# Both layer norms of a fused attention and mixture-of-experts layer: 16 small VectorE operations each made into two wide ones

## The reference

```python
# layernorm: (x - mean) / sqrt(var + 1e-5) over the 1024 channels
x = x + attn(layernorm(x))      # retention: (q k^T * decay) v, 16 heads of 64,
                                # group norm per head, plus silu(x w1), then @ w2
x = x + ffn(layernorm(x))       # router softmax, top 2 of 8 experts (all 8 computed,
                                # weights 0 elsewhere), plus a gated shared expert
```

## Time and profile before

| | us |
|---|---|
| median of 3 runs | 1963.68 (1962.49 to 1967.89) |
| the profiled execution | 1961.56 |
| its span, slowest core | 1959.8 |
| spans of the eight cores | 1945.3 to 1959.8 |
| PE busy / DVE busy / ACT busy | 1543.4 / 844.4 / 394.5 |

### The profile page before, as it was taken

One profiled execution on the slowest core, in us unless ns is written; L12 is line 12 of the kernel. 1 busy time (PEld: TensorE's weight loads), 2 busy tenths in 40 slices (PEclk: granted clock), 3 DMA queues, 4 the chain that ended last, 5 costly groups with the idle time before them and its releaser, 6 DMA issues.

```text
span 1959.8 us, 21098 instructions; the slowest of 8 cores (1945.3 to 1959.8 us)
## 1 busy us (share of the span) xinstructions
PE 1543.4 (79%) x7156; PEld 619.1 (32%) x7156; DVE 844.4 (43%) x1534; ACT 394.5 (20%) x771; POOL 24.9 (1%) x34
## 2 busy tenths in 40 slices
PE   0565677676576662999899999999999999999960
PEld 0121122122112111444343444444444444443420
DVE  0376666666657655222223333333333333332333
ACT  2433142233323111111121111111111111111100
POOL 1000000000000000000000000000000000000000
PEclk9755665575576565999999999999999999999985
DMA  9000020002000005200502202222220312223015
GB/s 145 2 1 1 0 43 1 0 1 44 1 0 22 1 1 108 44 1 1 86 1 44 44 1 47 40 44 44 43 44 1 53 34 43 44 44 65 1 61 175
DMA packets 41353, 67.27 MB, mean 34 GB/s; under 512 B 3858, under 2 KB 16530, under 8 KB 41250
## 3 DMA queue, kind: packets, MB, share of 16 engines
q0 software_dynamic: 26432, 48.65, 15.3%
q1 hardware_dynamic: 14818, 17.29, 2.7%
HBM read 101.96 MB, written 12.58 MB: 58 GB/s over the span
## 4 chain that ended last, share of the span: by engine, by line
PE 60%; DMA 15%; DVE 15%; issue 5%; DVEq 3%; ACT 2%; POOL 0%; ACTq 0%; SPq 0%; POOLq 0%
PE P L1206 18%; PE P L1238 17%; DMA we_sb<-we 11%; PE P L624 3%; PE P L867 3%; PE P L1071 3%; PE P L1124 3%; PE P L1082 3%; PE P L671 3%; DVE scr L363 2%; DMA xj<-x 2%; DMA x1rl<-x1s 2%; DVE s_sb L655 1%; DVEq L838 1%; PE P L426 1%
## 5 line engine op out<-in xcount | busy, mean ns | idle before, releaser
L1206 PE MATMUL P<-x2st,we_sb 128*128 128x512 bf16 x2048 | 454.2, 383 | 8.5 <-DMA we_sb<-we 8.5
L1238 PE MATMUL P<-htil,we_sb 128*128 128x512 bf16 x1984 | 435.9, 381 | 10.3 <-DMA we_sb<-we 10.3
L1217 ACT ACTIVATE hs_scr<-P 128x512 bf16<-128x512 f32 x256 | 152.9, 597 | 772.4 <-PE P L1206 772.4
L1250 DVE TENSOR_TENSOR acc<-acc,P 128x512 f32<-128x512 f32 x248 | 170.5, 687 | 256.9 <-PE P L1238 256.9
L1206 PEld LDWEIGHTS P<-x2st,we_sb 128*128 128x128 bf16 x2048 | 199.5, 99 | 255.5 <-issue 25.3
L1238 PEld LDWEIGHTS P<-htil,we_sb 128*128 128x128 bf16 x1984 | 194.2, 98 | 248.1 <-issue 17.1
L1224 DVE TENSOR_TENSOR htil<-hs_scr,bcomb 128x512 bf16<-128x512 bf16 x256 | 108.8, 425 | 353.9 <-ACT hs_scr L1217 353.9
L426 PE MATMUL P<-xlnj,w1a_sb 128*128 128x512 bf16 x256 | 79.4, 458 | 48.8 <-DVE xlnj L386 47.8
L624 PE MATMUL P<-qt,kst 64*128 64x512 bf16 x128 | 75.1, 599 | 33.8 <-ACT ktok L561 27.0
L648 DVE SCALAR_TENSOR_TENSOR s_sb<-P,gmn_sb,masks_sb 128x512 bf16<-128x512 f32 (+3 forms) x128 | 70.4, 550 | 72.1 <-PE P L630 65.0
L671 PE MATMUL P<-s_sb,vst 128*64 128x512 bf16 (+3 forms) x128 | 58.6, 458 | 29.3 <-DVE s_sb L655 28.5
(11 more groups left out here) (165 smaller groups left out, 1286.2 us busy)
## 6 DMA issues: line engine op xcount, KB each, us to landing
we_sb<-we POOLq DMA_DIRECT2D x16, 2048.0 KB, 14.6
out<-acc SPq DMA_DIRECT2D x4, 2048.0 KB, 8.0
xj<-x POOLq DMA_DIRECT2D x4, 1024.0 KB, 25.0
x1s<-xj SPq DMA_DIRECT2D x4, 1024.0 KB, 5.3
wgu_sb<-wgu POOLq DMA_DIRECT2D x1, 4096.0 KB, 30.2
x1rl<-x1s SPq DMA_DIRECT2D x4, 1024.0 KB, 10.3
w1a_sb<-w1a POOLq DMA_DIRECT2D x1, 2048.0 KB, 22.6
w2a_sb<-w2a POOLq DMA_DIRECT2D x1, 2048.0 KB, 35.3
```

The lines of the kernel that those rows point to most:

```text
L1206: last = e.matmul(bank[:, :], we1_sb[:, 1024 * k + 128 * f:1024 * k + 128 * f + 128], x2st[:, ST * k + 512 * j:ST * k + 512 * j + 512], st ...
L1217: e.activation(hs_scr[:, hsl:hsl + 512], bank[:, :], AF.Silu),
L1238: last = e.matmul(bank[:, :], we2_sb[:, 1024 * f + 128 * m:1024 * f + 128 * m + 128], htil[:, pslot + 512 * f:pslot + 512 * f + 512], star ...
L1250: e.tensor_add(acc[:, ST * m + 512 * pj:ST * m + 512 * pj + 512], acc[:, ST * m + 512 * pj:ST * m + 512 * pj + 512], bank[:, :]),
```

## The change

`ln_partB` is rewritten. Two new bf16 tiles in SBUF, `bcmu` and `bcrs` (128 x 512), take the spread mean and the reciprocal deviation: ACT copies the mean out of PSUM (new line 360), and DVE's reciprocal writes to `bcrs` in place of PSUM (new line 364). Instead of 16 operations on 512 columns there are two on 4096: one subtraction of `bcmu` (new line 384), one multiplication with `bcrs` (new line 387). The 512 columns of `bcmu` and `bcrs` are read eight times over, by a dimension of stride 0. All operands of both are bf16 in SBUF. LN1 subtracts into `xlnj` and multiplies in place; LN2 subtracts into the slot of `xlnj` that belongs to the same block and multiplies into `x2st`. `scr16` isn't used there any more. All eight marks that the function returns are that of the multiplication. The copy on ACT waits for the multiplication of the layer norm before, the LN2 subtraction for the last residual sum of its block.

```diff
@@ -203,6 +203,8 @@
     masks_sb = sb("masks_sb", [128, 1280], BF16)
     gmn4_sb = sb("gmn4_sb", [128, 64], F32)
     lgb = sb("lgb", [128, 320], F32)
+    bcmu = sb("bcmu", [128, 512], BF16)
+    bcrs = sb("bcrs", [128, 512], BF16)
     combT = sb("combT", [32, ST], BF16)
     eye_sb = sb("eye_sb", [128, 128], BF16)
     rout_sb = sb("rout_sb", [128, 72], BF16)
@@ -345,7 +347,8 @@
                 m_fin = p.do("scalar", fin, waits=[m_var, m_eps], mark=True)
                 return (st_b, m_fin, xoff, Mark("m_vector", m_var.value))
 
-            def ln_partB(ctx, bcA, bcB, dst_write, bc_waits=()):
+            def ln_partB(ctx, bcA, bcB, dst, bc_waits=()):
+                nonlocal prev_lnapply
                 st_b, m_fin, xoff = ctx[:3]
                 def bcast(e):
                     e.matmul(bcA[:, :], ones1_sb[0:1, :], st_b[0:1, 0:512],
@@ -354,40 +357,53 @@
                                     start=True, stop=True)
                 m_bc = p.do("tensor", bcast,
                             waits=[m_fin, m_ones1] + list(bc_waits), mark=True)
-                m_rec = p.do("vector", lambda e: e.reciprocal(
-                    bcB[:, :], bcB[:, :]), waits=[m_bc], mark=True)
-                marks = []
-                for c in range(8):
-                    def apply(e, c=c):
-                        sl = 1024 + (c % 2) * 512
-                        e.tensor_tensor(scr16[:, sl:sl + 512],
-                                        xj[:, xoff + 512 * c:xoff + 512 * c + 512],
-                                        bcA[:, :], ALU.subtract)
-                        e.drain()
-                        return dst_write(e, c, scr16[:, sl:sl + 512], bcB)
-                    marks.append(p.do("vector", apply, waits=[m_bc, m_rec],
-                                      mark=True))
-                return marks
-
-            def layernorm(m_src, stA, stB, bcA, bcB, dst_write, xoff=0,
+                m_evmu = p.do("scalar", lambda e: e.copy(bcmu[:, :], bcA[:, :]),
+                              waits=[m_bc, prev_lnapply], mark=True)
+                def rec(e):
+                    with nc.allow_low_precision(reason="bf16 rstd tile"):
+                        return e.reciprocal(bcrs[:, :], bcB[:, :])
+                m_rec = p.do("vector", rec, waits=[m_bc], mark=True)
+                mu_b = bcmu[:, :].unsqueeze(1).broadcast_to([128, 8, 512])
+                rs_b = bcrs[:, :].unsqueeze(1).broadcast_to([128, 8, 512])
+                if dst[0] == "ln1":
+                    xlo = dst[1]
+                    mid = xlnj[:, xlo:xlo + 4096].rearrange(
+                        "p (c t) -> p c t", t=512)
+                    out3 = mid
+                    guard = None
+                else:
+                    pj, pxo, guard = dst[1], dst[2], dst[3]
+                    xoff = pxo
+                    mid = xlnj[:, pxo:pxo + 4096].rearrange(
+                        "p (c t) -> p c t", t=512)
+                    out3 = x2st[:, :].rearrange("p (c t) -> p c t", c=8)[
+                        :, :, 512 * pj:512 * pj + 512]
+                in3 = xj[:, xoff:xoff + 4096].rearrange("p (c t) -> p c t", t=512)
+                def a1(e):
+                    with nc.allow_low_precision(reason="bf16 LN apply"):
+                        return e.tensor_tensor(mid, in3, mu_b, ALU.subtract)
+                def a2(e):
+                    with nc.allow_low_precision(reason="bf16 LN apply"):
+                        return e.tensor_tensor(out3, mid, rs_b, ALU.mult)
+                m_a1 = p.do("vector", a1, waits=[m_evmu, guard], mark=True)
+                m_a2 = p.do("vector", a2, waits=[m_a1, m_rec], mark=True)
+                prev_lnapply = m_a2
+                return [m_a2] * 8
+
+            def layernorm(m_src, stA, stB, bcA, bcB, dst, xoff=0,
                           bufs=None, first_waits=()):
                 ctx = ln_partA(m_src, stA, stB, xoff=xoff, bufs=bufs,
                                first_waits=first_waits)
-                return ln_partB(ctx, bcA, bcB, dst_write)
+                return ln_partB(ctx, bcA, bcB, dst)
 
             m_spill = None
+            prev_lnapply = None
             m_Minit = p.do("vector", lambda e: e.memset(Ms_f[:, :], 0.0), mark=True)
             m_Mcast = [m_Minit] * 8
             m_Mmm = [None] * 8
             m_vst_guard = [None] * 8
             m_kst_guard = [None] * 8
-            def mk_ln1_dst(xlo):
-                def ln1_dst(e, c, d1, rb, xlo=xlo):
-                    return e.tensor_tensor(
-                        xlnj[:, xlo + 512 * c:xlo + 512 * c + 512], d1,
-                        rb[:, :], ALU.mult)
-                return ln1_dst
-            ln1 = layernorm(m_x, P[6], P[7], P[6], P[7], mk_ln1_dst(0), xoff=0,
+            ln1 = layernorm(m_x, P[6], P[7], P[6], P[7], ("ln1", 0), xoff=0,
                             bufs=(ln1_f, ln1scr, ln1_b))
             m_x_cur = m_x
             m_ln2_prev = []
@@ -396,11 +412,8 @@
                 nonlocal pending_ln2B, m_ln2_prev, m_spill, m_x, m_x_next
                 ctx2, pj, pxo, pm_x1 = pending_ln2B
                 pending_ln2B = None
-                def ln2_dst(e, c, d1, rb, pj=pj):
-                    return e.tensor_tensor(
-                        x2st[:, ST * c + 512 * pj:ST * c + 512 * pj + 512],
-                        d1, rb[:, :], ALU.mult)
-                ln2 = ln_partB(ctx2, P[2], P[3], ln2_dst)
+                ln2 = ln_partB(ctx2, P[2], P[3],
+                               ("ln2", pj, pxo, pm_x1[7]))
                 m_ln2_prev = ln2
                 m_spill = spl.dma(lambda e, pj=pj, pxo=pxo: e.dma_start(
                     out=dx1s[:, :].rearrange("(c p) s -> p c s", p=128)
@@ -909,7 +922,7 @@
 
                 if j + 1 < nj:
                     ln1_next = ln_partB(ln1_ctx, P[0], P[1],
-                                        mk_ln1_dst(4096 * ((j + 1) % 2)),
+                                        ("ln1", 4096 * ((j + 1) % 2)),
                                         bc_waits=[m_om[6]])
 
                 if STAGE < 7:
```

## The result

The changed kernel takes 1914.2 us in the median; the kernel before, run beside it, 1966.2 in the median of all its runs and 1962.5 at the lowest. The ratio is 0.9738 (95% interval 0.9723 to 0.9754): 2.6% faster. In both, a few executions took 2.5 to 10% longer, with a lower clock on the cores of one die or both, and the ratio leaves these out. The prediction was 1922 (1911 to 1937). The profiled executions went from 1961.6 to 1914.3, 47.3 us less where 41.9 were forecast.

What follows compares the result with a forecast made beforehand. In the first part no engine is full; PE waits on all eight layer norms. Gains 6.1 + 8.9 + 8.9 + 10.5 + 7.5 = 41.9 us off 1961.6 give 1919.7, as a median 1922 us, range 1911 to 1937.

Steps and rivals of the forecast that it cites:

- The wide operation: Layer norms on DVE: one operation on 4096 bf16 SBUF columns takes 2.32 us (ends 1.9 to 3.4).
- A: Each layer norm on DVE: subtraction, multiplication and a gap take 4.7 us (3.9 to 6.9) in place of 12.25.
- Rival 1: Wide DVE operations: stride 0 costs the double rate, 4.4 us each, gain 17.5, total 1946 us; chance 0.08.
- The start of the gate: PE after LN1: gate matmuls start 8.25 us after the reciprocal's start, dense before at 15.85.
- DVE busy: DVE over the whole kernel: busy time down by 8 x 6.4 = 51 us.
- The gate's wait: PE's wait for LN1: some 8.3 us per block as one wait, 33 in all for 47.8.
- ACT's copy: Mean copied on ACT beside DVE's reciprocal: about 580 ns, showing only if ACT is late by more than 2.8 us.
- LN1, block 0: First layer norm: gate dense 7.6 us earlier, less 1.5 for seven matmuls now in the dense stretch; gain 6.1.
- LN2 hidden: Boundaries: LN2 ends 3.2 us before PE finishes the gate (1.6 at the last), so the v projection's wait goes.
- The three boundaries: Between blocks: LN1's 6.1 us plus the v projection's vanished wait; gains 8.9, 8.9 and 10.5 us.
- The last LN2: Last layer norm, standing alone: 12.25 us becomes 4.7; router, barrier and shared expert follow 7.5 us sooner.
- rival 2: Gate stage: the clock doesn't rise because PE idles 8.5 us beforehand; 34 us more, total 1956; chance 0.03.

Runs made afterwards that it cites:

- experiment 3: Changed kernel, but both wide layer norms read mean and reciprocal deviation from PSUM as fp32, without the ACT copy; 1946.6 us.
- experiment 1: Changed kernel with only LN1 wide; LN2 as in the kernel before (PSUM operands, eight pairs); 1929.8 us.
- experiment 5: Kernel before, with every gate matmul waiting for LN1's last chunk, so no seven single matmuls ahead of the dense stretch; 1974.0 us.
- experiment 11: Changed kernel with LN1's deviations inverted as a row (blocks 1 to 3), plus LN1 in two halves of 2048 columns; 1911.6 us lowest, 1923.0 profiled.
- experiment 2: Changed kernel with only LN2 wide; LN1 as in the kernel before; 1946.4 us.
- experiment 6: Kernel before, with LN2's part B (its spreading pair) put after gate output chunk 3 instead of 1; 1984.6 us.
- experiment 7: Kernel before, with LN2's `ln_tail` put ahead of LN1's part B at the block's end; 1967.6 us.
- experiment 4: Changed kernel's bf16 SBUF tiles, but both layer norms in eight pairs of 512 columns with drains instead of wide operations; 1925.2 us.
- experiment 8: Changed kernel with three small 512-column DVE operations between each LN1 reciprocal and subtraction, delaying the gate; 1917.0 us.
- experiment 9: Changed kernel with six small 512-column DVE operations between each LN1 reciprocal and subtraction, delaying the gate; 1934.1 us.

## Why the prediction was right, and which term was too small

- **The wide operation**: 2.32 forecast, 2.23 to 2.29 measured, so A = 4.6 to 4.7. Stride 0 doesn't cost the double rate: against the 425 ns of 512 columns, 4096 in 2260 are 0.51 ns per column, half of the 1.04 of the earlier trace rows. The Trainium skill ("Vector Engine (DVE) Microarchitecture Reference", section 5.1) had said that a row read again and again keeps two elements per cycle, and 4096 columns in 2260 ns agree. Rival 1 fell; experiment 3 shows what its world would have been (the gain 19.5 by the stages, 17.5 worked out).
- **The start of the gate**: 8.25 after the reciprocal forecast, 8.0 measured (223.42 to 231.45). DVE busy: 51 less forecast, 51.3 measured. The gate's wait 33 and 32.6. ACT's copy was never late: the 0.45 that DVE sat idle ahead of the last LN2's subtraction wasn't a wait for it, since it had ended 2.8 us before the reciprocal did.
- **LN1, block 0**: 6.1 forecast, 5.5 measured. The start came 7.8 sooner and the seven matmuls cost 2.3, not 1.5; a wait of 1.2 for ACT's silu stands in the gate now, and none stood there before.
- **LN2 hidden**: forecast to end 3.2 before the end of the gate, measured 3.0 (245.3 and 248.3). The v projection's wait is gone, as forecast; experiments 1 and 5 show it back (4.8 and 5.2) when LN2 is slow or late.
- **The three boundaries**: forecast 8.9, 8.9, 10.5, measured 11.6, 11.3, 11.6. This is the term that was too small. The step that failed is the assumption that the clock rises as long after the dense start as before: it gave a gate stage of 19.4 us, and 17.0 was measured, with the rise at 3.2 in place of 9. The prediction had put this possibility at 2 us sooner and 1 us per block; it was 6 sooner and 2.4. At boundary 3, where the clock had risen at 4.6 already before, 1.1 was missed. The rows of the kernel before held a sign of it: 57 dense matmuls took 15.4 us at block 0 and 17.9 at boundary 1, so the rise of 9 that was read at one boundary didn't hold for all gates.
- **The last LN2**: 7.5 forecast, 7.2 measured. The load of 4 MB stayed hidden; its slack before was 18.0 by the rows, not 17, and is 9.9 now.
- The attention stages between, from the v projection's start to the next layer norm's spreading pair, moved too, though nothing in them was changed: in the medians they are 0.4, 0.7 and 1.0 us longer in blocks 0 to 2 and 1.2 shorter in block 3. No step had foreseen this and no experiment explains it.

In sum: 2.7 + 2.4 + 1.1 at the boundaries, less 0.6 at block 0 and 0.3 at the last layer norm, is the 5.3 between 41.9 and 47.2. The other 0.5, up to the 47.7 by which the shared expert starts sooner, lies in the stages between and in the start of the first layer norm, 56 to 60 us into the span from core to core.

**What is behind the earlier rise.** The wide LN1 brings it, and taking the seven single matmuls away in the old kernel (experiment 5) brings the larger part of it, with no change on DVE: 5.4 to 5.8 in the medians, and 1.9 of the 2.4 us in the gate. So rival 2 had the sign of this effect wrong: PE standing idle ahead of the gate instead of doing a matmul each 1.54 us doesn't hold the clock down, it goes with an earlier rise.

The single cores say more than the medians. In the gate stages of all profiled kernels but experiment 11 the rise comes 2.6 to 6.0 us after the dense start or 8.2 to 9.4, and never in between. The late ones, 79 stages, are all at boundaries of the kernel before and of experiments 2, 6 and 7, out of 96 such stages, and in all 79 something breaks the dense stretch 3.9 to 4.0 us in: LN2's spreading pair, which stands behind 9 dense matmuls there, or in experiment 6 the wait for ACT. The 17 others rose at 2.6 to 4.6, before the break or during it. Where the stretch ran unbroken for at least 4.8 us, no rise was later than 6.0. That is so in the changed kernel and in experiment 5, where the pair stands behind 16 dense matmuls. It is also so in block 0 of the four kernels with late rises (2.7 to 5.9), which has the same seven matmuls 1.54 apart ahead but no LN2 in its gate. In experiment 4 the break, 3.3 to 3.6 us in, comes after the rise.

So the single matmuls ahead (the lead-in) alone don't put the rise off. They go with a late one where they leave only 9 matmuls for the dense stretch ahead of the pair. That the break is the cause fits every stage, but isn't shown: no run takes it away at a boundary and leaves the lead-in. Why cores with the same instructions differ stays open too. Over the whole range of early rises the gate took 16.6 to 17.6 us at the boundaries of the kernels whose 64 gate matmuls all stand in the dense stretch, so the gate would have been some 2 us shorter than the forecast 19.4 with any of them. That the rise came at 3.2 and not at 6 is worth less than 1 us per gate.

## What to carry to other kernels

Elementwise work that applies one row of factors to many chunks is worth turning into operations that are wide, all bf16 and all in SBUF, with the row read again by a stride of 0; here the SBUF tiles alone gave two thirds of the gain. Handing out chunks one by one, so that the next engine can start early, may be worth little: the seven early matmuls saved 2.3 and 1.5 us at two of four gates and nothing at the two others, while two halves (experiment 11) brought 4.9 in all. Look at whether what the engine does meanwhile makes its last matmul earlier, and at what then stands in its dense stretch. When a stretch starts after a different lead-in, give the time until its clock rises a range of its own (here 3 to 9 us), since it was the term of the sum that was most off.

## What the runs showed of the hardware that I had not expected

- The clock's rise came 2.9 to 3.2 us after the dense start in the medians of the changed kernel's boundaries, 5.4 to 6.0 in experiments 3 and 5, and 8.3 to 9.1 at most boundaries of the forms with the lead-in of seven matmuls 1.54 us apart. In each case the clock was at 1.2 GHz at the dense start, and the same 48 matmuls took 10.65 to 12.7 us.
- The same instructions at the same place of the same kernel can see either: 2.7 on one core and 8.8 to 9.4 on seven (experiment 2, boundary 1), 2.6 to 2.7 on five cores and 6.0 on three (experiment 1, boundary 3).
- A rise 1.6 us later cost only 0.1 us in the gate (experiments 8 and 9), since PE otherwise waits for ACT's silus: 0.65 us at boundary 1 of the changed kernel, and nothing there on the core shown of experiment 1, whose first 16 matmuls took 6.44 for 5.12.
- The reciprocal of 512 columns takes 3.36 us whether it writes fp32 to PSUM (3366 ns) or bf16 to SBUF (3358 ns); a copy of the same tile 0.69.
